# One decoder layer on one core: where the last group's weights are loaded, where VectorE adds the first residual, and a tail with an order of its own

## The reference

```
x = x + attn(layernorm(x))            # 128 heads, latent 64, rope part 64 wide, softmax over 128 keys, @ Wo
x = x + xattn(layernorm(x), ctx)      # 32 query heads, 8 key/value heads, rotary by position, softmax, @ Wo
x = x + ffn(layernorm(x)):
      result = h @ base_w.T + base_b
      weights, selected = top_k(h @ gate_w.T, 2); weights = softmax(weights)
      w_full = sum(one_hot(selected, 8) * weights)                       # 8 experts
      low = einsum('bsd,erd->ebsr', h, lora_A)                           # rank 16 each
      result + 2.0 * einsum('ebsr,eor,bse->bso', low, lora_B, w_full)
```

## Time and profile before

| what | us |
|---|---|
| median of 3 runs | 836.3 (836.21, 836.30, 837.79) |
| the profiled execution | 836.2 |
| its span, first to last instruction | 834.5 |
| PE busy | 795.2 (95% of the span) |
| DVE / ACT / POOL busy | 627.3 / 582.8 / 590.8 |
| mean granted PE clock | 0.997 of full speed |
| PE's share of the chain of waits that ended last | 82% |

### The profile page before, as it was taken

The page is one execution under the profiler, slowest core; times in us unless marked ns, Lnnn a source line. Parts: engine busy times, 40 slices in busy tenths (PEclk is TensorE's granted clock), DMA queues, the critical chain, the costliest instruction groups (busy, mean ns, idle before and its releaser), DMA issues.

```text
span 834.5 us, 17885 instructions
## 1 busy us (share of the span) xinstructions
PE 795.2 (95%) x5641; PEld 391.1 (47%) x5641; DVE 627.3 (75%) x1189; ACT 582.8 (70%) x1072; POOL 590.8 (71%) x535
## 2 busy tenths in 40 slices
PE   5999999999999999999999999999999888999986
PEld 3464444444444444444444444444434434545443
DVE  6767676676766888767788877688868868888755
ACT  8757777777777778777777777768765556556641
POOL 6967999999987888878888788868657334222110
PEclk9999999999999999999999999999999999999999
DMA  9345355534343333433334434452322000000001
GB/s 339 124 170 146 88 160 145 171 82 97 101 123 103 79 95 84 117 106 91 102 88 93 106 91 105 100 153 56 81 57 65 2 2 2 14 14 15 15 14 38
DMA packets 52177, 75.80 MB, mean 91 GB/s; under 512 B 10257, under 2 KB 34097, under 8 KB 51617
## 3 DMA queue, kind: packets, MB, share of 16 engines
q1 hardware_dynamic: 52128, 75.23, 32.8%
HBM read 38.69 MB, written 19.40 MB: 70 GB/s over the span
## 4 chain that ended last, share of the span: by engine, by line
PE 82%; DVE 7%; ACT 4%; issue 3%; SPq 2%; DMA 1%; POOL 0%; DVEq 0%; ACTq 0%
PE PS L1508 38%; PE PS L1442 7%; PE PS L1547 7%; PE PS L1580 7%; PE PS L1581 6%; PE PS L1595 5%; DVE xm L1281 1%; PE PS L1620 1%; PE PS L1741 1%; PE PS L1557 1%; PE PS L1707 1%; PE PS L1815 1%; PE PS L1629 1%; SPq L464 1%; PE PS L1748 1%
## 5 line engine op out<-in xcount | busy, mean ns | idle before, releaser
L1508 PE MATMUL PS<-XTh,W 128*128 128x512 f16 x1024 | 346.2, 379 | 0.0
L653 POOL TENSOR_TENSOR Pl<-PR,Ph 128x512 f16<-128x512 f32 x254 | 286.3, 1159 | 29.8 <-ACT Ph L935 29.8
L928 ACT ACTIVATE PR<-PS 128x512 f32<-128x512 f32 x256 | 152.8, 597 | 129.5 <-PE PS L1581 122.6
L1095 DVE TENSOR_REDUCE mneg<-PS 128x4 f16<-128x512 f32 x256 | 171.6, 685 | 34.7 <-PE PS L1547 33.0
L1508 PE MATMUL PS<-XTl,W 128*128 128x512 f16 x512 | 193.8, 379 | 0.0
L1083 DVE SCALAR_TENSOR_TENSOR QS<-PS,QC 64x512 f16<-64x512 f32 x256 | 175.4, 685 | 20.9 <-ACT QC L845 16.8
L845 ACT ACTIVATE QC<-PS 64x512 f16<-64x512 f32 x256 | 150.7, 589 | 9.2 <-PE PS L1508 4.3
L1508 PEld LDWEIGHTS PS<-XTh,W 128*128 128x128 f16 x1024 | 96.5, 97 | 118.8 <-issue 25.9
L935 ACT ACTIVATE Ph<-PR 128x512 f16<-128x512 f32 x256 | 139.2, 617 | 0.0
L1547 PEld LDWEIGHTS PS<-KC,QC 112*128 112x128 f16 x1024 | 78.4, 97 | 63.5 <-DVE mneg L1095 2.8
L1547 PE MATMUL PS<-KC,QC 112*128 112x128 f16 x1024 | 99.5, 219 | 0.8 <-ACT QC L845 0.7
(11 more groups left out here) (229 smaller groups left out, 1032.4 us busy)
## 6 DMA issues: line engine op xcount, KB each, us to landing
Wraw<-in_wqr SPq DMA_DIRECT2D x32, 512.0 KB, 4.8
QS<-QC SPq DMA_DIRECT2D x64, 256.0 KB, 3.1
head_outputs<-OS SPq DMA_DIRECT2D x256, 40.0 KB
q_content_parts<-stg SPq DMA_DIRECT2D x12, 256.0 KB, 2.9
k_content_parts<-stg SPq DMA_DIRECT2D x12, 256.0 KB, 3.1
QC<-q_content_parts SPq DMA_DIRECT2D x116, 24.0 KB
KC<-k_content_parts SPq DMA_DIRECT2D x29, 96.0 KB
xs<-in_x SPq DMA_DIRECT2D x8, 256.0 KB, 5.2
```

What stands on the lines that cost most here:

```text
L653: nc.gpsimd.tensor_tensor(Pl[:, 4 * j.s + b], PR[:, b], Ph[:, 4 * j.s + b], ALU.subtract).then_inc(s_pl, 1)
L928: nc.scalar.activation(PR[:, b, :], PS[:, bB[b % 2], :], ACT.Exp, scale=ATT_SCALE).then_inc(s_e, 1)
L1095: nc.vector.tensor_reduce(mneg[:, j.p, j.s, :, b], PS[:, bA[b % 2], :].rearrange("p (j k) -> p j k", j=GH), AX.X, ALU.max, negate=True).th ...
L1508: last = mm(PS[:, bQ[c], :], wt[:, j.w, k, c * P:(c + 1) * P], xt[:, k, sl], start=(i == 0), stop=(i == 3 * KT - 1))
```

## The change

Four edits. `w_in(NG - 1)` goes from the end of half 58's list on SP to right behind the store to `WD` in half 57. On DVE, `x1(LATER[u])` goes from behind the two `x_max` (and `norm_rows(1, ...)`) to ahead of `outputs_low` and of them. The steps of PE, ACT and DVE become functions that take a bank. Their loops stop at u = 31, and what follows is written out in an order of its own, with unit 31's output in bank 5, the last two gates in bank 1, batch 7's turn in bank 4, its output projection in bank 5, and its low-rank product alone in bank 4. Batch 7's low-rank values are scaled by the unnormalised weights, and the factor (2 over the sum, `mx`) is applied in the last addition. POOL's and SP's lists of this stage stay.

```diff
+        bG, bT7, bP7, bL7 = 1, 4, 5, 4
+        def o_bank(u):
+            return 1 if u < NU - 1 else 5
...
@@ sync, half()
                 if t == 1 and isinstance(g, int) and g == G0 - 1:
                     sp.wait_ge(s_ws, G0 + 1)
                     sp.dma_start(WD[0], W16[:, G0 % 2]).then_inc(s_wst, 16)
+                    w_in(NG - 1, G0 % 2)
@@ sync, late_half()
                 outputs(job(h - 4))
-                if h == LATE:
-                    w_in(NG - 1, G0 % 2)
@@ scalar, behind the loop, which now ends at NU
+            low_turned(B - 3)
+            x_out(NU - 1)
+            norm_high(2, B - 2, bF[0], s_f)
+            outputs_high(B - 1, bT7)
+            low_out(B - 2, bG)
+            gate_exp(B - 2)
+            norm_high(2, B - 1, bF[0], s_f)
+            low_turned(B - 2)
+            low_out(B - 1, bG)
+            gate_exp(B - 1)
+            low_turned(B - 1)
@@ vector, in the loop
                 if r == 1:
                     norm_low(2, b - 2, bF[0])
+                    x3(b - 3)
+                if u in LATER:
+                    x1(LATER[u])
+                if r == 2:
+                    outputs_low(b - 1, bF[0])
...
                 if 0 <= u + 2 < NU:
                     x_max(2 * u + 4)
                     x_max(2 * u + 5)
...
                 if r == 2:
                     norm_rows(1, b + 2)
-                if u in LATER:
-                    x1(LATER[u])
@@ vector, behind the loop
+            x_outputs(NU - 1)
+            norm_low(2, B - 2, bF[0])
+            outputs_low(B - 1, bT7)
+            gate_first(B - 2)
+            x2(B - 1, bP7)
+            norm_stats(2, B - 1)
+            norm_rows(2, B - 1)
+            gate_last(B - 2)
+            norm_low(2, B - 1, bF[0])
+            x3(B - 3)
+            gate_first(B - 1)
+            v = B - 1
+            dve.wait_ge(s_gy, B)
+            link(nc.vector.scalar_tensor_tensor(ex[:], rank[:], 1.5, ex[:], ALU.is_lt, ALU.mult))
+            l = low[:, v % 2, 0:E * R].rearrange("p (e r) -> p e r", r=R)
+            nc.vector.tensor_tensor(l, l, ex[:, :, None].to_broadcast([P, E, R]), ALU.mult).then_inc(s_lw, 1)
+            link(nc.vector.tensor_reduce(mx[:], ex[:], AX.X, ALU.add))
+            link(nc.vector.reciprocal(mx[:], mx[:]))
+            link(nc.vector.tensor_scalar(mx[:], mx[:], SCALING, None, ALU.mult))
+            x3(B - 2)
+            dve.wait_ge(s_o2, B + 1)
+            dve.wait_ge(s_xb, B)
+            link(nc.vector.scalar_tensor_tensor(xs[:, v, :], PS[:, base_bank(v), :], 1 / WS, xs[:, v, :], ALU.mult, ALU.add))
+            dve.wait_ge(s_f, B)
+            nc.vector.scalar_tensor_tensor(xs[:, v, :], PS[:, bL7, :], mx[:], xs[:, v, :], ALU.mult, ALU.add).then_inc(s_x3, 1)
@@ tensor
+            def base(v, n):
+                if n == 0:
+                    pe.wait_ge(n_th[2], v + 1)
+                    pe.wait_ge(s_xl, 9)
+                if n == 2:
+                    pe.wait_ge(n_tl[2], v + 1)
+                xt, wt = ((Ah2, bwh), (Ah2, bwl), (Al2, bwh))[n]
+                for k in range(KT):
+                    last = mm(PS[:, base_bank(v), :], xt[:, v % 2, k], wt[:, k], start=(n == 0 and k == 0),
+                              stop=(v == B - 1 and n == 2 and k == KT - 1))
+                return last
+
+            def lora(v):
+                pe.wait_ge(s_lT, v + 1)
+                pe.wait_ge(s_ffn, 80)
+                mm(PS[:, base_bank(v) if v < B - 1 else bL7, :], lowT[:, v % 2], lb_sb[:], start=(v == B - 1), stop=True
+                   ).then_inc(s_f, 1)
@@ tensor, behind the loop
+            pe.wait_ge(s_kq, NU)
+            pe.wait_ge(s_xme, NU)
+            low_turn(B - 3)
+            x_back(NU - 2)
+            x_weigh(NU - 1)
+            take(bF[1], s_x3, B - 2)
+            base(B - 3, 0)
+            x_back(NU - 1)
+            norm_turn(2, B - 2, bF[0])
+            outputs_turn(B - 1, bT7)
+            gate(B - 2, bG)
+            project_outputs(B - 1, bP7)
+            base(B - 3, 1)
+            base(B - 3, 2)
+            lora(B - 3)
+            base(B - 2, 0)
+            norm_turn(2, B - 1, bF[0])
+            base(B - 2, 1)
+            low_turn(B - 2)
+            pe.wait_ge(s_ge, B - 1)
+            gate(B - 1, bG)
+            base(B - 2, 2)
+            lora(B - 2)
+            for n in range(3):
+                last = base(B - 1, n)
+            last.then_inc(s_o2, 1)
+            low_turn(B - 1)
+            lora(B - 1)
```

More of the change, by code:

```diff
@@ L1019, in query_high @@
                                      ACT.Copy).then_inc(s_qst, 1)
-            for u in range(FIRST, LAST):
+            for u in range(FIRST, NU):
                 b, r = (u + 1) // KT, (u + 1) % KT
@@ L1025, in _ @@
                     query_high(b + 1, 1)
[L1026 to L1034, removed]
+                if r == 1:
+                    low_turned(b - 3)
+                if r == 3:
+                    gate_exp(b - 2)
                 if r == 1:
                     norm_high(2, b - 2, bF[0], s_f)
[L1037 to L1049, removed]
+                if r == 2:
+                    low_out(b - 2, bF[1])
+                    outputs_high(b - 1, bF[0])
                 if r == 3:
@@ L1669, in _, with low_turn, gate, project_outputs @@
                     output(v, T)
-            def base(v):
-                pe.wait_ge(s_xl, 9)
-                parts(base_bank(v), Ah2[:, v % 2], Al2[:, v % 2], bwh, bwl, 0, DM, stop=False)
+            def base(v, n):
[14 more added lines that the diff above has]
+                   ).then_inc(s_f, 1)
+            def low_turn(v):
+                pe.wait_ge(s_lw, v + 1)
+                if v >= 1:
+                    pe.wait_ge(s_lT, v)
+                nc.tensor.transpose(PS[:, 0, 3 * S:], low[:, v % 2, 0:E * R], ident[:]).then_inc(s_lt, 1)
+            def gate(v, bank):
+                pe.wait_ge(n_th[2], v + 1)
+                pe.wait_ge(s_xl, 5)
+                parts(bank, Ah2[:, v % 2], Al2[:, v % 2], agh, agl, 0, AG, (n_tl[2], v + 1)).then_inc(s_lg, 1)
+            def project_outputs(v, bank):
+                pe.wait_ge(s_oT, v + 1)
+                pe.wait_ge(s_xl, 4)
+                parts(bank, O2h[:, v % 2], O2l[:, v % 2], woh, wol, 0, DM, (s_oTl, v + 1)).then_inc(s_o2, 1)
             last_read = {}
@@ L1809, in _ @@
                         v = b - 3
-                        if v < B - 2:
-                            take(bF[1], s_x3, v + 1)
-                            base(v)
-                        pe.wait_ge(s_lT, v + 1)
-                        pe.wait_ge(s_ffn, 80)
-                        mm(PS[:, base_bank(v), :], lowT[:, v % 2], lb_sb[:], start=False, stop=True).then_inc(s_f, 1)
+                        take(bF[1], s_x3, v + 1)
+                        for n in range(3):
+                            base(v, n)
+                        lora(v)
                     norm_turn(2, b - 2, bF[0])
@@ L1819, in _ @@
                         v = b - 2
-                        pe.wait_ge(n_th[2], v + 1)
                         take(bF[1], s_ge, v + 1)
-                        pe.wait_ge(s_xl, 5)
-                        parts(bF[1], Ah2[:, v % 2], Al2[:, v % 2], agh, agl, 0, AG, (n_tl[2], v + 1)).then_inc(s_lg, 1)
-                        if v == B - 1:
-                            base(v)
+                        gate(v, bF[1])
                 if r == 3:
```

102 lines of the change are left out of this document (60 added, 42 removed).

## The result

The changed kernel takes 827.2 us (median of 4 runs, 826.69 to 828.87) against 837.0 for the kernel before in the same comparison (836.21 to 840.0): ratio 0.989, interval 0.987 to 0.990. The forecast was 825.0 in a range of 823.2 to 828.4. The direction and the places were right. The time is 2.2 us above the forecast; the gain is 9.9 us where 11.3 were forecast, since a fourth run of the kernel before (840.0) moved its median from 836.3 to 837.0. The profiled execution took 826.78 us with a span of 824.5.

What follows compares the result with a forecast made beforehand. TensorE's in-order queue (82% of the chain) plus its standstills in head attention, cross attention and tail bound the kernel. Gains 1.75 + 5.4 + 4.16 = 11.3 from 836.2 give 824.9, with 0.1 to the median 825.0 us; range 823.2 to 828.4.

Steps and rivals of the forecast that it cites:

- outside the span: Execution time beyond the profiled span: 1.7 us (span 834.5, time 836.2), with no change in the sum.
- weight load, halves 58 and 59: Head attention: half 59 falls 2.36 us to 8.73, half 58 pays 0.6; gain 1.75, ends 0.25 and 2.36.
- x1, u = 5 to 16: Cross attention: `x1` ahead of the maxima removes PE's waits for a PSUM bank; gain 5.4, ends 3.7 and 6.0.
- tail: From 807.80: packed order brings batch 7's projection to 812.54 and the end to 830.33; gain 4.16, range 3.2 to 4.6.
- The rival of the jammed queue: Head attention: moved load jams the stores behind it, maxima of job 56 come 2 us late; price 1.5, 826.5; chance 0.14.
- x1 at u = 5: Cross attention: the whole 2.04 us wait goes, and with it the clock's fall over two groups, 1.68.
- u = 9: Cross attention: rough scores wait for the KQ copy, starting at 693.72 instead of 694.18; gain 0.46.
- the clock falls elsewhere: Rival: clock falls at another wait, such as the 1.76 us rope wait at 689.50; price 1.7, 826.7; chance 0.16.
- u = 12 and 16: Cross attention, priced at u = 11 and 15: base product no longer starts 0.66 and 0.58 late; gain 1.24.
- Before 807.80 nothing changes: Start of the tail: claimed no change ahead of the turn of `low` at 807.80.
- The rival of half the gain: Tail: late norm chain or `x_outputs` use up the covering base products; 2 us instead of 4.2, 827.2; chance 0.08.
- The scaling "at no cost": End of the tail: scaling of batch 7's low rank moves into the last addition at no cost.

Runs made afterwards that it cites:

- x1_only: Kernel before with only the residual addition `x1` moved ahead of `outputs_low` and the two `x_max`: 831.91 us, ratio 0.993.
- tail_only: Kernel before with only the written-out tail, its banks and its divided last addition: 834.87 us, ratio 0.9961.
- rope_early: `load_behind_q` with VectorE's rope of batch 3 moved ahead of the two `x_max` of u = 7: 826.08 us.
- combined: `load_behind_q` plus `rope_early`, `fewer_waits`, GpSimd's last bias add held, and batch 7 finished as before the change: 823.84 us, ratio to before 0.984.
- load_behind_q: Changed kernel with group 31's weight load issued in half 58 behind the q copy, thus behind the maxima of job 56: 826.28 us.
- fewer_waits: `load_behind_q` without repeating TensorE's waits on loaded weights, fulfilled for good after their first time: 825.81 us.

## Why the prediction was nearly right, step by step

The range held, and the three places and the direction were right. But 827.2 lies outside the 824 to 826.2 that had the highest chance, and all three signs that the forecast had named as "wrong" came in the profile: a wait in half 58 above 1 us (1.23), a low clock before the last addition (686 to 688), and a wait inside the tail's packed block (0.15). The measured time is near the prices of single rivals (826.5, 826.7, 827.2), yet no rival holds the term that failed, the time outside the span. So the range held partly by luck.

The terms, forecast against the profiled executions (changes of start to start between the same two groups):

| term | forecast | measured |
|---|---|---|
| weight load, halves 58 and 59 | -1.75 | -1.27 |
| x1, u = 5 to 16 | -5.4 | -4.5 |
| tail | -4.16 | -4.07 |
| outside the span | 0 | +0.56 |
| up to half 58 | 0 | -0.14 |
| sum | -11.3 | -9.4 |

- *Weight load.* Half 59 fell to 8.74 as forecast (8.73). The price in half 58 was mis-sized: 1.08 instead of 0.6. The maxima were issued 0.65 later (552.38 instead of 551.73), and then up to 2.3 us passed to the landing instead of 1.7. The term was read from one execution; by the four and three profiles compared above, the same move gains 1.3 to 3.1. The rival of the jammed queue had the maxima 2 us late; they landed about 1.25 late, and the jam is as long with the load in front of it (4.37) as without (4.38, 4.34).
- *x1 at u = 5.* 3.71 gained at the norm turn (679.04 to 674.01, less the 1.32 had before), 3.72 forecast: the wait of 2.04 and the two slow groups. The rows of before, and that of u = 9 for the next point:

```profile
679.04 0.61 PE L1758 MATMUL PS<-ident,pn 128*128 128x128 f32 x4
...
694.18 0.40 PE L1707 MATMUL PS<-KQ 48*128 48x128 f16 x8
```

- *u = 9.* Here a rival came true, in this execution: "the clock falls elsewhere", at the very wait I had named. Instead of +0.46 the place lost 0.17 (689.32 against 694.18). The step was right, as `x1_only` shows (0.56 us for KQ). But I had priced a fall at 1.7 and it cost 0.63 (0.46 and 0.17). From the norm turn to the last group of the gate the slow stretch lost 1.2 us (4.48 instead of the 3.25 of `x1_only`). About half of that came back, since `x1_only` then waits 0.56 for KQ and this execution doesn't.
- *u = 12 and 16.* 0.65 and 0.60 gained, 0.66 and 0.58 forecast. The four places add up to 4.8; the 4.5 of the table also holds 0.1 lost ahead of u = 5 and the 0.2 of the next point.
- *The start of the tail.* "Before 807.80 nothing changes" was wrong by 0.2: the turn of `low` starts 0.42 instead of 0.22 after what went before, in every kernel with the tail edit. I take it for the two waits that now stand in front of it; they weren't tried alone.
- *The tail.* 4.59 to the projection (4.74 forecast) and 12.93 to the last turn (12.74). The 0.15 wait in it comes from GpSimd's add holding up a VectorE operation, which I hadn't counted. The rival of half the gain was wrong by mechanism, though `tail_only` shows 2.7 us: 0.67 more lies outside its span, and its profile takes 24.1 us from the turn of `low` to the end instead of 22.6, with the fall of the clock shown above.
- *The scaling "at no cost".* It cost 0.14.
- *Outside the span.* I took the 1.7 us as a constant. This is the term that failed: +0.56 in the profiled execution, +0.7 as a median, the largest single miss beside the clock.
- *The starting point.* The forecast started from 836.2, the median of three runs being 836.3. With more runs the kernel before stands at 837.0 to 837.6, so the forecast began about a microsecond low, and a gain of 11.3 would have given 826. Against these medians the gain is 9.6 to 9.9.

Together these misses are 0.48 + 0.9 + 0.09 + 0.56 - 0.14 = 1.9 us, which is 824.9 against 826.78.

What stays open: what decides whether the clock falls behind a given wait, what places the last instruction transfer, and how much of each median gain is the clock.

## What to carry to other kernels

Count the time outside the span as a term: a change that writes out loops or adds waits can lengthen the engine's code, and here one more block of it cost 0.67 us, which leaving out long fulfilled waits gave back. A transfer that must land soon should stand ahead of the large load on the same queue, not behind it: with the load moved behind the maxima TensorE waited 0 to 0.4 us for them, and 0.8 to 1.2 with it ahead. Read a wait from several executions before pricing its removal: halves 58 and 59 of one and the same order took 20.15 to 21.49 us. Price a fall of the clock by what lies behind it: two packed groups of 512-wide matmuls lost 1.7 us, and the small products at u = 8 and 9, with a wait behind them that came anyway, 0.63.

## What the runs showed of the hardware

- A VectorE operation on 128x8 took 0.87 us instead of 0.23 when it came while GpSimd added 128x512, and ended with that add (eight profiles of eight).
- The clock's fall behind one wait isn't a property of the wait: the same 1.76 us at the rope was followed by 1.2 GHz in two of seven profiles. Of the two kernels that took this wait away, `rope_early` had a fall elsewhere (800.03) and `combined` none up to the end; `tail_only` had two (676.45 and 809.57).
- The kernel's instruction fetch shows in the time: 16 KB more behind the end went with 0.67 us, at a span that differed by 0.2 (`load_behind_q`, `fewer_waits`).
